# Transposed probabilities of the relation layers move into the attention's two PSUM banks

## The chip, the cores and the metric

One core of a Trainium2 chip runs the whole program. The metric is the device time of one execution in microseconds. The engines are TensorE (PE), VectorE (DVE), ScalarE (ACT), GpSimd (POOL) and SyncE (SP), which issues most transfers.

## What is computed

The input is 128 graphs of 128 nodes with 256 features and a 0/1 adjacency matrix each. They pass through one attention block and two relation layers:

```python
nx = ln(x); q, k, v = nx @ wq + bq, nx @ wk + bk, nx @ wv + bv      # 8 heads of 32
attn = softmax(q @ k.T / sqrt(32) + where(adj > 0, 0.1 * adj * adj, -inf))
x1 = x + (attn @ v) @ wo + bo
x = x1 + gelu(ln(x1) @ w1 + b1) @ w2 + b2                           # hidden width 1024
for l in range(2):                                                  # relation layers
    q, k = x @ Wq[l].T + bq[l], x @ Wk[l].T + bk[l]                 # width 128
    a = softmax(where(adj == 0, -1e10, q @ k.T / sqrt(128)))        # then 0 where adj == 0
    x = ln(x + (a @ x) @ Wc[l].T) * g[l] + b[l]
```

Most dense products are made as three matmuls of 16-bit halves (high by high, high by low, low by high), to come near fp32.

## The kernel before

Four graphs make a group, so there are NG = 32 groups. The work on a group is cut into steps named stage.step: N (first layer norm), Q (projections q0, q1, k0, k1, v0, v1), A (attention: S scores, max, exp, PT transposed probabilities, AV, each for graph 0 to 3, then oT, wo, and st, rs, xh of the second norm), M (MLP: mT, up0 to up7, lo, down0 to down7, x2), C0 and C1 (the two relation layers: xT, q, k, S, max, ex, xW, PT, PV, st, rs, xh, af).

It is a software pipeline. Every engine has a list of steps, each with an offset of groups ("C1.PT-4" is that step for the group four behind), and `run` goes through the list once for each group; after the last, a second list (`TENSOR_END` and so on) drains the pipeline. Each engine keeps strictly to its list, and waits on semaphores for what others make. The lists are all that sets the order of the work.

PSUM has eight banks. Banks 0 and 1 are the attention's (psA): A.S writes 8 heads of scores there, VectorE takes them away with the bias added (L872, d_S), A.PT transposes the exps into the same two banks (L1304), and ScalarE (L673) and VectorE (L880, d_PT) take those away as a high and a low half; A.wo writes them as well (taken away by L902, d_x1). Banks 2 and 3 serve Q, AV and up, 4 and 5 the MLP's output, and 6 and 7 the relation layers: q and S in bank 6, k in 7, xW and PV as rows in both.

In a relation layer, xW is x @ Wc and is copied to cW by ScalarE (L715). The exps (L709) are made in place in cs; PT transposes cs by TensorE (L1360) into bank 6 + l, ScalarE copies that back to cs (L719), and PV multiplies cs by cW (L1366). So either PT needs cW copied away first. VectorE scales and adds the residual in C0.PV and C1.PV (L955).

What each step of TensorE must wait for so that its banks are free stands in `freed` calls: freed(g, (signal, behind, per, k)) waits until `signal` has come k times for the group `behind` places before g. Other lines that the text names: L688 gelu (L691 its high half, L334 its low half, by VectorE for even and POOL for odd pieces), L667 exps of the attention, L681 high half of mT, L921 x2, L749 and L754 statistics, L762 normalised rows, L544 and L546 the reciprocal root on POOL, L551 row additions on POOL, L1297 A.S, L1348 C.S, and L327 to L329, the three matmuls of a product of any kind. rot is what A.wo and M.up read, cT what C.q, C.k and C.xW read; SyncE's transfers transpose into them.

## Time and profile before

| | us |
|---|---|
| median of 3 runs | 2076.52 |
| lowest, highest | 2076.26, 2077.35 |
| the profiled execution's own time | 2075.52 |
| its span | 2073.3 |
| mean granted TensorE clock | 0.976 |

The profile is one execution; times in its rows are from the span's start. TensorE is busy for 1868.7 of 2073.3 us, VectorE for 1701.3, ScalarE for 1563.1 and POOL for 925.4. A row of a timeline gives start, duration, engine, line, operation and tiles; in brackets is the engine's idle time before it and what ended it. Matmuls overlap by about 0.17 us, so a TensorE step makes room for the next one somewhat before its row ends.

### The profile page before, as it was taken

The numbers are of one execution on the slowest core, as the hardware profiler recorded it, in microseconds if no ns is written. First come the engines' busy times: TensorE is split into PE (matmuls) and PEld (weight loads), VectorE is DVE, ScalarE is ACT, GpSimd is POOL, SyncE is SP. The second block draws the span as 40 slices with busy tenths as digits, with TensorE's granted clock in tenths as the row PEclk, the third lists the DMA queues.
The fourth block names the chain that finished last, engine by engine and source line by source line (L and its number), as shares of the span: only waits on it lengthen the run. The fifth ranks groups of instructions, "written<-read, shape, count | busy, mean of one in ns | idle before, by whom it ended". The sixth has DMA issues, their size and how long they took to land.

```text
span 2073.3 us, 44187 instructions
## 1 busy us (share of the span) xinstructions
PE 1868.7 (90%) x15704; PEld 1347.0 (65%) x15704; DVE 1701.3 (82%) x3402; ACT 1563.1 (75%) x2996; POOL 925.4 (45%) x1168
## 2 busy tenths in 40 slices
...
PEclk8788899999999999999999999999999999999998
...
DMA packets 441657, 192.45 MB, mean 93 GB/s; under 512 B 347808, under 2 KB 416416, under 8 KB 441440
## 3 DMA queue, kind: packets, MB, share of 16 engines
...
q8 instruction: 128, 2.10, 0.4%
q0 software_dynamic: 544, 0.80, 0.2%
...
## 4 chain that ended last, share of the span: by engine, by line
PE 60%; ACT 18%; DVE 10%; POOL 5%; issue 4%; DMA 1%; SPq 1%; ACTq 0%; DVEq 0%; POOLq 0%
PE ps L327 16%; PE ps L329 16%; PE ps L328 16%; PE ps L1304 6%; ACT area L667 4%; PE ps L1366 3%; DVE st L749 2%; ACT L688 2%; DVE area L762 2%; ACT cs L709 2%; POOL hid_l L334 2%; DVE area L902 2%; ACT L709 2%; POOL rs L546 2%; POOL ve L544 2%
## 5 line engine op out<-in xcount | busy, mean ns | idle before, releaser
L544 POOL TENSOR_TENSOR ve<-mv,eps_cols 128x4 f32<-128x4 f32 x128 | 64.1, 500 | 738.5 <-DVE mv L754 738.5
L667 ACT ACTIVATE area<-area,nmax 128x128 f32<-128x128 f32 x1024 | 312.6, 390 | 17.0 <-DVE nmax L877 16.2
L327 PE MATMUL ps<-w_h,hid_h 128*128 128x256 f16 x1024 | 279.5, 273 | 12.1 <-POOL hid_l L334 12.1
L334 POOL TENSOR_TENSOR hid_l<-area,hid_h 128x512 f16<-128x512 f32 x128 | 156.4, 1222 | 279.1 <-ACT hid_h L691 279.1
L328 PE MATMUL ps<-w_l,hid_h 128*128 128x256 f16 x1024 | 279.3, 273 | 0.0
L329 PE MATMUL ps<-w_h,hid_l 128*128 128x256 f16 x1024 | 279.2, 273 | 0.0
L688 ACT ACTIVATE area<-ps,b_col 128x512 f32<-128x512 f32 x256 | 176.1, 688 | 41.0 <-PE ps L329 37.9
L327 PE MATMUL ps<-rot_h,w_h 128*128 128x512 f16 x512 | 198.5, 388 | 8.4 <-ACT area L688 5.3
L328 PE MATMUL ps<-rot_l,w_h 128*128 128x512 f16 x512 | 198.0, 387 | 0.0
L329 PE MATMUL ps<-rot_h,w_l 128*128 128x512 f16 x512 | 197.9, 387 | 0.0
L880 DVE SCALAR_TENSOR_TENSOR pT<-ps,pT 128x1024 f16<-128x1024 f32 x128 | 156.1, 1220 | 20.1 <-ACT pT L673 20.1
L551 POOL TENSOR_TENSOR x<-x,cb_row 128x256 f32<-128x256 f32 x240 | 167.3, 728 | 4.7
L858 DVE SCALAR_TENSOR_TENSOR qk<-ps,bqk_col,qk 128x512 f16<-128x512 f32 x128 | 95.6, 747 | 84.2 <-ACT qk L656 84.2
L691 ACT CAST hid_h<-area 128x512 f16<-128x512 f32 x256 | 158.2, 618 | 8.2
L872 DVE SCALAR_TENSOR_TENSOR area<-ps,biasA 128x1024 f32<-128x1024 f32 x128 | 154.9, 1211 | 5.3 <-PE ps L1297 5.3
L877 DVE TENSOR_REDUCE nmax<-area 128x8 f32<-128x1024 f32 x128 | 155.4, 1214 | 2.2
L673 ACT ACTIVATE pT<-ps 128x1024 f16<-128x1024 f32 x128 | 130.3, 1018 | 25.3 <-PE ps L1304 25.3
L1304 PE MATMUL ps<-ident,area 128*128 128x128 f32 x1024 | 138.3, 279 | 11.4 <-ACT area L667 6.7
L1366 PE MATMUL ps<-area,cs 128*128 128x256 f32 x512 | 125.2, 388 | 20.3 <-ACT cs L719 19.1
L1304 PEld LDWEIGHTS ps<-ident,area 128*128 128x128 f32 x1024 | 117.9, 144 | 33.6 <-issue 17.4
L697 ACT CAST sC_h<-area 128x1024 f16<-128x1024 f32 x32 | 33.4, 1045 | 137.8 <-DVE area L921 137.8
L546 POOL TENSOR_TENSOR rs<-ve,minus_half 128x4 f32<-128x4 f32 x128 | 132.7, 1036 | 10.0
...
## 6 DMA issues: line engine op xcount, KB each, us to landing
...
rot_h<-sA_h SPq DMA_TRANSPOSE x64, 2.8
rot_l<-sA_l SPq DMA_TRANSPOSE x64, 2.7
```

The lines of the kernel that those rows point to most:

```text
L327: pe.matmul(dst, lh, rh, start=start, stop=False, **kw)
L328: pe.matmul(dst, lh, rl, start=False, stop=False, **kw)
L329: return pe.matmul(dst, ll, rh, start=False, stop=stop, **kw)
L334: eng.tensor_tensor(hid_l[:, c % RING, :], hidden[:, c % 2, :], hid_h[:, c % RING, :], ALU.subtract).then_inc(done, 1)
L546: pool.tensor_tensor(rs[:, n], ve[:, n], minus_half[:, :], ALU.pow).then_inc(p_rs[n], 1)
L551: last = pool.tensor_tensor(dst[:, b], src[:, b], row, op)
L667: last = act.activation(sc[:, b % 2, h], sc[:, b % 2, h], ACT.Exp, bias=nmax[:, b, h:h + 1])
L688: act.activation(hidden[:, b % 2, :], psUp, ACT.Gelu, bias=b1_col[:, b:b + 1], scale=1.0 / W_SCALE).then_inc(a_gelu, 1)
L691: act.copy(hid_h[:, b % RING, :], hidden[:, b % 2, :]).then_inc(a_hi, 1)
L880: dve.scalar_tensor_tensor(pT16[:, b % 2, 1], psA_heads, P_SCALE, pT16[:, b % 2, 0], ALU.mult, ALU.subtract).then_inc(d_PT, 1)
L1304: last = pe.transpose(psA_heads[:, h], sc[:, b % 2, h], ident[:, :])
L1366: last = pe.matmul(rows_of(l, g)[:, b], cs[:, l, b], places(l, g)["cW"][:, b], start=True, stop=True)
```

## The change

The transposed probabilities of both relation layers go into bank l (0 or 1), the attention's, in place of bank 6 + l; a new helper `turned` gives the place to TensorE's transpose and ScalarE's copy. C0.PT and C1.PT then wait for the attention's last use of the bank, and no more for cW; A.wo and A.S1 wait for the copies out of it (a_cPT). For C1.PT in the steady lists that last use is A.S0 of the group four ahead of it (d_S), for C0.PT it is A.PT3 of the group two ahead (d_PT). All ten order lists are written anew, and the waits of TensorE with them. One piece of VectorE's preparation for the first group moves from Q.mA to A.S0.

```diff
--- before.py
+++ after.py
@@ -49,66 +49,67 @@
 
 
 
-TENSOR = ["M.down2-2", "M.up6-2", "Q.q0+0", "A.S3-1", "C0.S-3", "Q.q1+0", "A.AV0-1", "M.down3-2",
-          "A.PT2-1", "A.AV1-1", "M.down4-2", "Q.k1+0", "A.AV2-1", "A.PT3-1", "C0.xW-3", "A.AV3-1",
-          "M.up7-2", "C0.PT-3", "M.down5-2", "C0.PV-3", "M.down6-2", "M.down7-2", "A.wo-1",
-          "C1.q-4", "C1.k-4", "C1.S-4", "Q.v1+0", "Q.v0+0", "A.S0+0", "C1.xW-4", "C1.PT-4",
-          "A.S1+0", "M.up0-1", "C1.PV-4", "M.up1-1", "A.PT0+0", "M.up2-1", "M.down0-1", "M.up3-1",
-          "M.down1-1", "C0.q-2", "A.S2+0", "M.up4-1", "Q.k0+1", "C0.k-2", "A.PT1+0", "M.up5-1"]
-SCALAR = ["M.up2-2", "A.PT0-1", "M.up3-2", "A.exp1-1", "M.up4-2", "Q.k0+0", "A.PT1-1", "M.up5-2",
-          "C0.q-3", "C0.k-3", "M.up6-2", "Q.q0+0", "A.exp2-1", "Q.q1+0", "C1.xT-4", "A.PT2-1",
-          "A.exp3-1", "Q.k1+0", "A.PT3-1", "C0.ex-3", "C0.xW-3", "A.oT-1", "C0.PT-3", "M.up7-2",
-          "C0.xT-2", "C1.q-4", "C1.k-4", "Q.v1+0", "M.mT-1", "C1.ex-4", "C1.xW-4", "A.exp0+0",
-          "C1.PT-4", "M.up0-1", "Q.v0+0", "M.up1-1", "N.xT+1"]
-VECTOR = ["C1.max-5", "M.mT-2", "A.S0-1", "A.max0-1", "M.mC-3", "Q.v1-1", "N.st+0", "C0.st-4",
-          "A.S1-1", "N.xh+0", "M.lo0-2", "A.max1-1", "N.xT+0", "C1.PV-5", "A.PT0-1", "Q.v0-1",
-          "C1.st-5", "M.lo2-2", "A.S2-1", "A.max2-1", "C0.xh-4", "Q.k0+0", "C1.xh-5", "M.lo4-2",
-          "A.PT1-1", "Q.q0+0", "C0.S-3", "A.S3-1", "A.AV0-1", "A.max3-1", "C0.max-3", "Q.q1+0",
-          "A.AV1-1", "A.PT2-1", "C1.xT-4", "Q.k1+0", "A.AV2-1", "A.PT3-1", "A.AV3-1", "A.oT-1",
-          "M.lo6-2", "Q.mA+0", "C0.PV-3", "M.x2-2", "A.wo-1", "A.st-1", "C0.xT-2", "C1.S-4",
-          "A.xh-1"]
-GPSIMD = ["N.rs+1", "C0.rs-3", "M.lo1-1", "C1.rs-4", "M.lo3-1", "C1.af-4", "A.x1b-1", "M.lo5-1",
-          "C0.af-3", "M.lo7-1", "N.xb+0", "A.rs+0"]
-SYNC = ["C1.xT-4", "A.oT-1", "Q.stk+0", "M.ldC-2", "N.ld+1", "M.mT-1", "C0.xT-2", "Q.ldA+1",
-        "N.xT+1", "C1.sto-4"]
+TENSOR = ["M.up6-2", "M.down3-2", "A.S3-1", "A.AV0-1", "C0.S-3", "Q.q1+0", "A.AV1-1", "A.PT2-1",
+          "M.down4-2", "Q.k1+0", "A.AV2-1", "A.PT3-1", "C0.xW-3", "A.AV3-1", "C0.PT-3", "M.up7-2",
+          "M.down5-2", "C0.PV-3", "M.down6-2", "M.down7-2", "A.wo-1", "C1.k-4", "Q.v1+0", "C1.q-4",
+          "Q.v0+0", "C1.S-4", "A.S0+0", "C1.xW-4", "C1.PT-4", "A.S1+0", "M.up0-1", "C1.PV-4",
+          "A.PT0+0", "M.up1-1", "C0.k-2", "M.up2-1", "A.S2+0", "M.up3-1", "M.down0-1", "M.down1-1",
+          "M.up4-1", "M.down2-1", "Q.k0+1", "A.PT1+0", "M.up5-1", "C0.q-2", "Q.q0+1"]
+SCALAR = ["A.exp0-1", "M.up0-2", "A.PT0-1", "M.up1-2", "N.xT+0", "M.up2-2", "C1.xT-4", "M.up3-2",
+          "A.exp1-1", "M.up4-2", "Q.k0+0", "C0.k-3", "A.PT1-1", "M.up5-2", "Q.q0+0", "C0.q-3",
+          "M.up6-2", "A.exp2-1", "Q.q1+0", "A.PT2-1", "A.exp3-1", "Q.k1+0", "A.PT3-1", "C0.ex-3",
+          "C0.xW-3", "C0.PT-3", "A.oT-1", "M.up7-2", "C1.k-4", "C0.xT-2", "Q.v1+0", "C1.q-4",
+          "Q.v0+0", "M.mT-1", "C1.ex-4", "C1.xW-4", "C1.PT-4"]
+VECTOR = ["M.mT-2", "A.S0-1", "A.max0-1", "C0.xh-4", "N.st+0", "M.mC-3", "A.S1-1", "C1.PV-5",
+          "M.lo0-2", "N.xh+0", "A.PT0-1", "A.max1-1", "Q.v0-1", "N.xT+0", "C1.st-5", "M.lo2-2",
+          "A.S2-1", "Q.k0+0", "A.max2-1", "C1.xh-5", "M.lo4-2", "A.PT1-1", "Q.q0+0", "A.S3-1",
+          "A.AV0-1", "A.max3-1", "C0.S-3", "A.AV1-1", "Q.q1+0", "C0.max-3", "A.PT2-1", "C1.xT-4",
+          "A.AV2-1", "Q.k1+0", "A.PT3-1", "M.lo6-2", "A.AV3-1", "A.oT-1", "C0.PV-3", "Q.mA+0",
+          "M.x2-2", "C0.st-3", "A.wo-1", "A.st-1", "C0.xT-2", "Q.v1+0", "A.xh-1", "C1.S-4",
+          "C1.max-4"]
+GPSIMD = ["M.lo1-1", "C1.rs-4", "M.lo3-1", "N.xb+1", "C1.af-4", "A.x1b-1", "M.lo5-1", "C0.af-3",
+          "M.lo7-1", "C0.rs-2", "A.rs+0", "N.rs+2"]
+SYNC = ["N.ld+0", "M.ldC-3", "M.mT-2", "C0.xT-3", "N.xT+0", "Q.ldA+0", "C1.sto-5", "C1.xT-4",
+        "A.oT-1", "Q.stk+0"]
 
 QK = ("q0", "q1", "k0", "k1")
...
+TENSOR_END = ["A.AV0-1", "A.S3-1", "C0.S-3", "M.down3-2", "C0.xW-3", "A.PT2-1", "M.down4-2",
+              "A.AV1-1", "M.up6-2", "A.AV2-1", "A.PT3-1", "C1.k-4", "C1.q-4", "A.AV3-1", "M.up7-2",
+              "C0.PT-3", "M.down5-2", "C0.PV-3", "M.down6-2", "C1.S-4", "M.down7-2", "A.wo-1",
+              "C1.xW-4", "C1.PT-4", "C1.PV-4", "C0.k-2", "C0.q-2", "M.up0-1", "C1.k-3", "M.up1-1",
+              "C0.S-2", "M.up2-1", "M.down0-1", "M.up3-1", "C0.xW-2", "M.up4-1", "M.down1-1",
+              "C0.PT-2", "M.down2-1", "M.up5-1", "C1.q-3", "M.up6-1", "M.down3-1", "M.up7-1",
...
@@ -281,6 +282,9 @@
 
         def keys_of(l, g, n):
             return bank_of(l, g, n).rearrange("p (b k) -> p b k", b=B)
+
+        def turned(l):
+            return ps[:, l, :].rearrange("p (b k) -> p b k", b=B)
 
         def rows_of(l, g):
             first = ROWS_LAST[l] if number(g) == NG - 1 else places(l, g)["bank"]
@@ -716,7 +720,7 @@
                         elif what == "PT":
 
                             need(act, t_cPT[l], g, 1, 1)
-                            act.copy(cs[:, l], keys_of(l, g, l)).then_inc(a_cPT[l], 1)
+                            act.copy(cs[:, l], turned(l)).then_inc(a_cPT[l], 1)
 
             run(SCALAR, SCALAR_END, iteration)
 
@@ -777,7 +781,7 @@
                     assert made[0] == BQK_MADE, made[0]
                     prep(dve.tensor_copy(bv_rep, bv_col[:, :].unsqueeze(2).broadcast_to([P, KC, P])))
                     prepped()
-                elif step == "Q.mA":
+                elif step == "A.S0":
                     lows(HALVES_QKV, HALVES_QKVO)
                     dve.wait_ge(ld_vec, 16 * NVEC)
                     prep(dve.tensor_copy(cb_rep, cln_col[:, 1, :].unsqueeze(2).broadcast_to([P, KC, P])))
...
+                    elif step == "C0.PT":
+                        freed(g, (d_PT, -2, 4, 4), (d_x1, -1, 1, 1), (a_cPT[0], 1,
+                              1, 1))
...
                     elif step == "A.wo":
+                        freed(g, (a_cPT[0], 2, 1, 1), (d_PT, 0, 4, 4))
                         freed(g, (d_PT, 0, 4, 4))
...
                     elif step == "C1.PT":
-                        freed(g, (a_cW[1], 0, 1, 1))
+                        freed(g, (d_S, -4, 4, 1), (d_x1, -3, 1, 1), (a_cPT[1], 1, 1,
+                              1))
                     elif step == "A.S1":
                         freed(g, (d_S, 0, 4, 1))
+                        freed(g, (a_cPT[1], 4, 1, 1), (d_S, 0, 4, 1))
...
                     elif step == "C1.PV":
                         freed(g, (a_cW[1], 0, 1, 1))
-                        freed(g, (a_cPT[1], 0, 1, 1))
+                    elif step == "A.PT0":
+                        freed(g, (d_S, 0, 4, 2))
...
+                    elif step == "A.S2":
+                        freed(g, (d_PT, 0, 4, 1))
...
@@ -1357,7 +1363,7 @@
                         elif what == "PT":
                             for b in range(B):
                                 need(pe, a_cexp[l], g, B, b + 1)
-                                last = pe.transpose(keys_of(l, g, l)[:, b], cs[:, l, b], ident[:, :])
+                                last = pe.transpose(turned(l)[:, b], cs[:, l, b], ident[:, :])
                             last.then_inc(t_cPT[l], 1)
                         elif what == "PV":
                             need(pe, a_cPT[l], g, 1, 1)
```

In the end lists (the rest is left out above) C1.k, C1.q and C1.S of the fourth last group stand before A.wo of the last, and C1.PV of it and C0.k and C0.q of the second last group before M.up0 of the last; before, they all stood behind.

## Rows read from the trace of the kernel before

**Rows 1.** The page: busy us and shares; clock granted, in tenths
```profile
PE 1868.7 (90%) x15704; PEld 1347.0 (65%) x15704; DVE 1701.3 (82%) x3402; ACT 1563.1 (75%) x2996; POOL 925.4 (45%) x1168
...
PEclk8788899999999999999999999999999999999998
```

**Rows 2.** Chain of work in order of time: start, us, what
```profile
1063.39 1.24 DVE area L902
...
1123.83 1.24 DVE area L902
```

**Rows 3.** TensorE's waits, 400 to 1800: us in total, times, longest
```profile
PE ps L1360 <- ACT area L715: 40.0, 23, 2.0
PE ps L1348 <- ACT ck L702: 20.9, 24, 0.9
PE ps L1366 <- ACT cs L719: 13.9, 23, 0.7
PE ps L327 <- POOL hid_l L334: 9.4, 23, 0.4
```

**Rows 4.** Timeline of TensorE: start, us, line, operation, idle before
```profile
1075.36 0.66 PE L1360 MATMUL ps<-ident,cs 128*128 128x128 f32 x4 [1.73 <-ACT area L715]
...
1076.30 0.38 PE L327 MATMUL ps<-rot_h,w_h 128*128 128x512 f16 x1
...
1078.37 0.89 PE L1366 MATMUL ps<-area,cs 128*128 128x256 f32 x3 [0.61 <-ACT cs L719]
...
1088.94 0.61 PE L1297 MATMUL ps<-qkS 96*128 96x128 f16 x8
...
1121.01 0.27 PE L327 MATMUL ps<-wo_h,rot_h 128*128 128x256 f16 x1
```

**Rows 5.** Timeline of ScalarE, same group
```profile
1070.39 1.05 ACT L681 CAST sA_h<-area 128x1024 f16<-128x1024 f32 x1 [0.52 <-DVE area L762]
...
1071.46 1.28 ACT L709 ACT_TABLE_LOAD   x1
...
1077.55 0.57 ACT L719 COPY cs<-ps 128x512 f32<-128x512 f32 x1
...
1080.15 0.62 ACT L691 CAST hid_h<-area 128x512 f16<-128x512 f32 x1
...
1101.54 2.45 ACT L667 ACTIVATE area<-area,nmax 128x128 f32<-128x128 f32 x8
```

**Rows 6.** Timeline of VectorE, same group
```profile
1061.05 1.23 DVE L921 SCALAR_TENSOR_TENSOR area<-ps,area 128x1024 f32<-128x1024 f32 x1
...
1063.39 1.23 DVE L902 SCALAR_TENSOR_TENSOR area<-ps,xin 128x1024 f32<-128x1024 f32 x1 [1.12 <-PE ps L329]
...
1068.98 1.38 DVE L762 TENSOR_SCALAR area<-area,mv,rs 128x256 f32<-128x256 f32 x4 [0.31 <-POOL rs L546]
...
1072.62 1.22 DVE L872 SCALAR_TENSOR_TENSOR area<-ps,biasA 128x1024 f32<-128x1024 f32 x1
...
1081.98 0.68 DVE L334 TENSOR_TENSOR hid_l<-area,hid_h 128x512 f16<-128x512 f32 x1
...
1087.23 1.21 DVE L880 SCALAR_TENSOR_TENSOR pT<-ps,pT 128x1024 f16<-128x1024 f32 x1
```

**Rows 7.** Timeline of POOL, same group
```profile
1066.66 1.09 POOL L544 TENSOR_TENSOR ve<-mv,eps_cols 128x4 f32<-128x4 f32 x1 [4.72 <-DVE mv L754]
...
1077.93 0.20 POOL L544 TENSOR_TENSOR ve<-mv,eps_cols 128x4 f32<-128x4 f32 x1 [9.09 <-DVE mv L754]
...
1097.16 3.16 POOL L551 TENSOR_TENSOR x<-x,cg_row 128x256 f32<-128x256 f32 x4 [3.43 <-DVE x L762]
...
1118.28 1.35 POOL L334 TENSOR_TENSOR hid_l<-area,hid_h 128x512 f16<-128x512 f32 x1 [4.63 <-ACT hid_h L691]
```

**Rows 8.** The page: transfer issues, with us from issue to landing
```profile
rot_l<-sA_l SPq DMA_TRANSPOSE x64, 2.7
```

**Rows 9.** Timeline of TensorE in the last groups
```profile
1979.91 1.54 PE L1360 MATMUL ps<-ident,cs 128*128 128x128 f32 x4 [3.01 <-ACT cs L709]
```

174 lines of the change are left out of this document (76 added, 98 removed), and 26 rows, old and new, of tables (SCALAR_END, VECTOR_END).

## The prediction

> **What bounds the kernel now.** I read the page first: TensorE is busy 90% of the span and its granted clock is at 90% or more of full speed (the 2.4 GHz level) from the sixth of 40 slices to the last but one, so TensorE sets the pace [rows 1]. Then the chain of work: the residual after the output projection (L902, step A.wo of VectorE) comes once per group of four graphs, 60.44 us apart [rows 2]. There are 32 groups, so 31 such distances, of which I count 30 as steady. Then TensorE's waits over 1400 us, 23 groups: 84.2 us in four kinds, 3.66 us a group [rows 3]. Each ends a pipeline that has to fill again (about 0.16 us, the overlap of two neighbours), so 4.3 of 60.44 us are lost and 56.1 us are TensorE's own work. The largest wait, 1.73 us, is the one this change attacks: the transposes of the second relation layer (C1.PT, L1360) stand behind ScalarE's copy of cW (L715), because they share its bank [rows 3, 4].
>
> In what follows T is the time from the start of A.wo on TensorE, 1060.57 in the trace; the next one starts at 1121.01, T 60.44 [rows 4]. TensorE's own pace: the six 512-column matmuls of M.up0 start at 1076.30 and end 0.61 before 1078.37, the last of them lasting 0.38, so 0.216 us from start to start; the 24 of 256 columns of A.wo are done 2.8 us after 1121.01, when L902 starts, 0.109 each [rows 2, 4]. So q, k, up, Q.* take 1.30, a down or half of Q.v 1.31, A.wo and xW 2.62; from start differences, A.S 0.45, C.S 0.95, C.PT 0.50, A.PT 0.9, AV 0.60, PV 1.80.
>
> **The change, part by part.** No instruction is added or removed; all go by other lists, and two orderings change their banks.
>
> 1. *C1.PT into bank 1.* It no longer waits for cW, but for the evacuation of A.S0 (L872). And A.S1, which writes bank 1, now waits for ScalarE's copy of cs (L719). Queued behind A.S1 on TensorE is all the rest, M.up0 first. So the old wait (1.73) and the PV wait (0.61) are exchanged for a wait at A.S1, whose release is: transpose copy of A.xh 1.05, table load 1.28, four exps 1.56, cW 0.9, cs copy 0.57 [rows 5]. (The four exps and cW: from the table load's end, 1072.74, to the cs copy at 1077.55 are 4.81, less 2.35 for the eight exps of A.exp0 in between: 2.46.) Today M.up0 starts at T 15.73 (1076.30), after 12.8 of own work [rows 4].
>
> 2. *C0.st put between M.x2 and A.wo on VectorE.* Today VectorE idles 1.12 there [rows 6]. x2 can start at T 0.20 (last down ends, plus 0.04) instead of 0.48, since C0.PV is now ahead of Q.mA; x2 takes 1.14 to the next start, the statistics 1.41+0.14+0.30. A.wo goes to T 3.19 instead of 2.82: +0.37. From A.wo to A.xh are 5.59 us (1063.39 to 1068.98), statistics and the two POOL steps, 1.09 and the rsqrt behind it [rows 6, 7]; same neighbours, so A.xh at 8.78. C1.S and C1.max now follow it (0.69+0.03+0.61 before M.mT, which needs ScalarE's copy at 11.23 anyway): M.mT 11.40, A.S0 12.55. On ScalarE: copy 10.19 to 11.23, exps from 12.54, cW 14.1, cs copy 15.0 to 15.56, A.S1 15.62, M.up0 **16.07**, against 15.73. PV then goes at 17.37 without waiting (today 17.80), so 0.4 is gained here.
>
> 3. *A.S2 earlier.* It waits for VectorE's share of A.PT0 (L880), in a list that now reads A.S0, max0, C0.xh, N.st, mC, A.S1, C1.PV, lo0, N.xh, A.PT0. Today the stretch from A.S0 (1072.62) to the end of N.xh (1081.98) takes 9.36 [rows 6]; out of it go Q.v1 (0.60) and C0.st (1.81), into it come C0.xh (1.29, as N.xh), C1.PV (1.97), lo0 (0.60) and A.PT0 itself (1.21): 12.02. So 12.55 + 12.02 = 24.57, and with 0.05 to 0.14 of signal A.S2 starts at 24.62 to 24.71. TensorE would be there at 16.07 + 8.0 = 24.07 (up0, PV, PT0, up1, C0.k, up2). That is a new wait of 0.6, where today A.S2 comes four steps later (T 28.37) and finds its banks free.
>
> 4. *From A.S2 to exp2.* TensorE's own work to M.up6 is 13.1: up6 at 37.8. ScalarE: up6 ends 39.25, gelu 0.69 and cast 0.62 (with the gap 1.35: from the table load after the cs copy, over at 1079.42, to 1080.77), table load 1.28, exp2 2.45 with small gaps [rows 5]: exp2 done at 44.4, today 43.4 (1103.99). Then PT2 waits 0.15 (exp to TensorE takes 0.14), PT2's copy 45.5, exp3 to 48.95 and **A.PT3 at 49.1**, today 48.35. TensorE alone would be there at 48.65: a wait of 0.45.
>
> 5. *The end of the group.* From PT3 TensorE has xW, AV3, C0.PT, up7, down5, PV, down6, down7: 11.5 us, so A.wo at 60.65 if nothing waits. C0.PT moved ahead of up7 and its copy ahead of A.oT: the copy ends at 54.5, A.oT 55.45, table load 56.75, gelu and cast 58.1, lo7 on POOL (1.16 to 1.35, rows 7) 59.3 to 59.5. Today's wait before down7 (0.41) shrinks to 0 to 0.2. A.wo at **60.8**. So 60.44 becomes 60.8: +0.35 a group, ends +0.0 (if every hand-off falls at its short end and lo7 is hidden, with the PT0 step short) and +0.6.
>
> 6. *Moves that cost nothing.* N.xb goes to POOL's idle 3.4 us before C1.af [rows 7]; should that cover go, lo5 would come 2.78 late and down5 still has 6 us. ldC behind N.ld on SyncE, and N.xT later on VectorE: its transpose lands near 30.5, read at 31.7. The transpose that M.up0 reads takes 2.7 to land [rows 8]: issued near 12.85, it is there at 15.6, before 16.07; this is the nearest cover of all, and if it went, up0 would come later by what it overshoots. Six table loads a group, as before. DVE's preparation moves from Q.mA to A.S0, once.
>
> 7. *The last groups.* The end lists put C1.k, C1.q, C1.S(-4) ahead of A.wo(-1), and PV(-4), C0.k, C0.q(-2) ahead of M.up0(-1), a place where TensorE waits 3.01 for exps [rows 9]. From up0 to the last down the own work falls from 35.1 to 30.2 us; up0 starts some 2 us later, since C0.k needs C1.PV evacuated. I take −3, ends −6 and +2. The start: 0, ends ±2.
>
> Sum against the profiled execution, span 2073.3 and time 2075.52: 30 groups x 0.35 = +10.5, −3: +7.5, so 2083.0. The median shown, 2076.52, lies 1.0 above that execution; for it I say **2084**.
>
> **A rule weighed.** The row first: the same POOL addition on 128x4 took 1.09 us beside VectorE's C0.xT and 0.20 elsewhere [rows 7]; it ended when C0.xT did. The Trainium skill, page "SBUF — State Buffer", section "Who interferes with whom", says that whichever of the two engines issues first holds the shared ports for the whole instruction and the other blocks, here for a VectorE operation with two SBUF inputs; the trace agrees with 1.09 against 0.20. What that gives where POOL is first is the fourth rival.
>
> **The rivals.**
> *Faster.* The freed bank pays: VectorE's list is not late at A.S2, because x2 and the statistics hide in the 1.12 of idle time and the PT0 step is reached by T 24.0. The place is A.wo of VectorE, the price 0.37 plus the wait of 0.6; it decides if A.S2 starts under 24.1. Then 60.0 a group: 30 x −0.44 − 3 = −16: 2060.5. For it: waits of 1.73 and 0.61 do vanish. Against it: the chain x1 to A.xh has no slack.
> *Even.* The waits only trade places, 60.44 stays, and the end gives −3: 2073.5. For it: 4.3 lost today, 4.4 to 4.8 by my sum, less than my hand-offs can tell apart.
> *It doesn't do what it says:* C1.PT still stands behind cW's time, since A.S1 waits for the copy that ScalarE makes after cW. That is in the forecast.
> *Much slower.* lo1 on POOL is issued ahead of N.xh on VectorE (T 22.95 against 22.07 by my sum; it decides 0.9 earlier) and holds it for 1.16: A.S2 at 25.8, 30 x 1.45 − 3 = +40: 2117.
>
> **How the numbers follow.** Forecast 0.50, faster 0.20, even 0.24, much slower 0.06. The forecast's own range is 2077 to 2092; with even and half of faster I give 2062 to 2092, which leaves 0.10 below and 0.08 above. Within 0.2% (4 us, about what can be told from no change) lies 0.14 of the forecast's 0.50 and 0.15 of even's 0.24, the other 0.09 being faster: faster 0.29, same 0.29, slower 0.42.
>
> **What would show it.** Right: L902 60.7 to 60.9 apart; C1.PT's wait on L715 gone; waits of L1297 on L719 (A.S1) of about 2 and on L880 (A.S2) of 0.4 to 0.7; L1304 on L667 0.3 to 0.5; L902 on VectorE with hardly any idle time before it. Wrong: A.S2 without a wait (step 3), a distance under 60.4, or a last stretch that is not shorter (step 7).

## The result and the profile after

The changed kernel takes 2094.27 us (median of 3 runs, 2094.0 to 2098.02) against 2076.52: a ratio of 1.0091, 95% interval 1.0075 to 1.0107. It is slower by 17.75 us, where +7.5 was forecast and 2092 was the top of the range. Its profiled execution took 2094.0 us, span 2091.1, at nearly the same mean granted clock (0.974 against 0.976). That mean hides two places where TensorE's clock stands at half (0.50 of full, the 1.2 GHz level): once for 3.4 us among the middle groups, where the kernel before has none, and for 10.2 us instead of 3.4 in the last groups. Both come up below. The page, with the clock in tenths as in [rows 1]:

```profile
PE 1892.6 (91%) x15704; PEld 1354.8 (65%) x15704; DVE 1671.9 (80%) x3402; ACT 1566.5 (75%) x2996; POOL 928.6 (44%) x1168
...
PEclk8699899999999999999999999999999999999998
```

The code has moved by 4 to 6 lines: L902 is now L906, L1360 is L1366 (C.PT), L1297 is L1303 (A.S), L1304 is L1310 (A.PT), L1366 is L1372 (C.PV), L872 is L876, L880 is L884, L719 is L723 and L327 to L329 are L331 to L333. The chain of work (start, us, what) answers [rows 2]:

```profile
641.84 1.12 DVE area L906
702.76 1.12 DVE area L906
...
1191.42 1.19 DVE area L906
1246.89 2.73 DMA rot_l<-sA_l
1252.57 1.24 DVE area L906
```

The first pair is 60.92 us apart. The second is 61.15 apart, and here a transfer has come into the chain: the low half of the transpose that A.wo reads. In the chain of the kernel before it does not occur between 500 and 1700 us. TensorE's waits from 400 to 1800 us answer [rows 3]:

```profile
PE ps L1303 <- issue: 25.1, 23, 1.1
PE ps L331 <- DVE cs L940: 23.4, 23, 1.5
PE ps L1310 <- DVE area L876: 7.4, 22, 0.7
PE ps L1310 <- ACT area L671: 7.3, 23, 0.3
PE ps L1303 <- DMA qkS<-qk: 5.5, 9, 0.9
PE ps L1366 <- DVE area L876: 4.4, 23, 0.2
PE ps L331 <- DMA rot_l<-sA_l: 4.4, 9, 0.9
```

C1.PT's wait for the copy of cW (40.0 us) is gone, as intended. In its place A.S1 waits 1.09 us in each group; the profile names no releaser ("issue"), but in the group of A.wo at 699.43, whose other rows stand further below, ScalarE's cs copy ends at 715.01 and A.S1 starts at 715.11:

```profile
714.45 0.56 ACT L723 COPY cs<-ps 128x512 f32<-128x512 f32 x1
```

C1.xW waits for VectorE's evacuation of C1.S (L940), A.PT0 for that of A.S1, and in 9 of 23 groups A.wo waits for its transpose. All in all TensorE waits for fewer microseconds, but more often: 77.7 us in 133 waits, against 84.2 us in 93 [rows 3]. Its busy time is 23.9 us longer with the same instructions, so part of what is lost stands inside its busy rows: A.wo at 1127.45, for instance, starts 0.38 us behind the matmul before it, where neighbours in that row are 0.11 apart, and no wait is listed.

I took the starts of A.wo from the traces (31 distances). By them the 17.5 us between the two last A.wo starts (1966.0 and 1983.5) are: 1.1 before the first A.wo, 186.6 to 183.2 = −3.4 over the first three distances, +19.1 over the next 27, +0.7 in the last. So the middle groups are 0.71 longer each (mean 60.47 to 61.18). The commonest distance goes from 60.44 to 60.91, so 0.47 or 0.48 of this is the base, and 0.23 come from groups above it. (In the changed kernel only 7 of 27 groups stand at 60.91 to 60.93; four are shorter.) From the last A.wo to the end it is 107.3 and 107.7: the last groups gave nothing.

### The profile page after: what moved, and what is told of

The parts are those of the page before. It is cut to its first block, busy times and chain, and to the rows that moved or that the text cites. A ratio compares the mean times of both kernels' runs of the same rounds, so it can differ in the third digit from the quotient of the medians.

```text
span 2091.1 us, 44128 instructions
## 1 busy us (share of the span) xinstructions
PE 1892.6 (91%) x15704; PEld 1354.8 (65%) x15704; DVE 1671.9 (80%) x3402; ACT 1566.5 (75%) x2996; POOL 928.6 (44%) x1168
## 4 chain that ended last, share of the span: by engine, by line
PE 53%; DVE 25%; issue 7%; ACT 6%; POOL 3%; DMA 3%; SPq 2%; DVEq 0%; ACTq 0%; POOLq 0%
PE ps L331 14%; PE ps L333 14%; PE ps L332 14%; PE ps L1310 6%; DVE st L753 5%; ACT area L671 4%; DVE area L876 3%; DVE area L766 2%; DVE area L906 2%; PE ps L1372 2%; DVE xh L959 2%; DMA rot_l<-sA_l 2%; DVE xh L766 2%; POOL rs L550 2%; POOL ve L548 2%
## 5 line engine op out<-in xcount | busy, mean ns | idle before, releaser
L338 POOL TENSOR_TENSOR hid_l<-area,hid_h 128x512 f16<-128x512 f32 x128 | 149.3, 1166 | 302.3 <-ACT hid_h L695 302.3
L331 PE MATMUL ps<-w_h,hid_h 128*128 128x256 f16 x1024 | 279.4, 273 | 1.0 <-POOL hid_l L338 1.0
L333 PE MATMUL ps<-w_h,hid_l 128*128 128x256 f16 x1024 | 279.1, 273 | 0.0
L331 PE MATMUL ps<-rot_h,w_h 128*128 128x512 f16 x512 | 197.0, 385 | 10.4 <-ACT area L692 3.4
L333 PE MATMUL ps<-rot_h,w_l 128*128 128x512 f16 x512 | 196.8, 384 | 0.0
L706 ACT ACTIVATE ck<-ps,cb_col 128x512 f32<-128x512 f32 x61 | 41.6, 682 | 206.3 <-PE ps L333 206.3
L884 DVE SCALAR_TENSOR_TENSOR pT<-ps,pT 128x1024 f16<-128x1024 f32 x128 | 156.3, 1221 | 40.5 <-ACT pT L677 40.5
L555 POOL TENSOR_TENSOR x<-x,cb_row 128x256 f32<-128x256 f32 x240 | 179.8, 780 | 4.7
L876 DVE SCALAR_TENSOR_TENSOR area<-ps,biasA 128x1024 f32<-128x1024 f32 x128 | 156.0, 1219 | 20.6 <-PE ps L1303 17.2
L1310 PE MATMUL ps<-ident,area 128*128 128x128 f32 x1024 | 141.7, 283 | 25.1 <-DVE area L876 13.1
L331 PE MATMUL ps<-cw_h,cT_h 128*128 128x256 f16 x488 | 133.3, 273 | 29.4 <-DVE cs L940 29.4
L1310 PEld LDWEIGHTS ps<-ident,area 128*128 128x128 f32 x1024 | 116.9, 145 | 49.5 <-DVE area L876 26.9
L1303 PE MATMUL ps<-qkS 96*128 96x128 f16 x1024 | 81.1, 224 | 67.3 <-issue 30.6
```

What stands on the lines that cost most here:

```text
L331: pe.matmul(dst, lh, rh, start=start, stop=False, **kw)
L333: return pe.matmul(dst, ll, rh, start=False, stop=stop, **kw)
L338: eng.tensor_tensor(hid_l[:, c % RING, :], hidden[:, c % 2, :], hid_h[:, c % RING, :], ALU.subtract).then_inc(done, 1)
L555: last = pool.tensor_tensor(dst[:, b], src[:, b], row, op)
L876: dve.scalar_tensor_tensor(sc[:, b % 2], psA_heads, 1.0 / QK_SCALE, biasA[:, b].unsqueeze(1).broadcast_to([P, H, P]), ALU.mult, ALU.add).t ...
L884: dve.scalar_tensor_tensor(pT16[:, b % 2, 1], psA_heads, P_SCALE, pT16[:, b % 2, 0], ALU.mult, ALU.subtract).then_inc(d_PT, 1)
```

## The experiments

T is again the time from A.wo's start. In the texts put down ahead of each run, T1 is the theory under test, R1 and R2 its rivals. Line numbers of the experiments are off by up to 6 from those above. The table holds all kernels; the distance is that of A.wo's starts over the 27 middle groups, commonest and mean.

| kernel | us | ratio to before, 95% | distance |
|---|---|---|---|
| before | 2076.52 | 1 | 60.44; 60.47 |
| changed | 2094.27 | 1.0091 (1.0075 to 1.0107) | 60.91; 61.18 |
| e1_oT_first | 2110.55 | 1.0178 (1.0155 to 1.0201) | none; 61.88 |
| e2_st_late | 2159.75 | 1.0405 (1.0391 to 1.0419) | 62.79; 63.32 |
| e3_both | 2190.92 | 1.0556 (1.0534 to 1.0579) | none; 64.95 |
| e4_end_swap | 2093.38 | 1.0081 (1.0065 to 1.0097) | 60.91; 61.21 |
| e5_lists_old_banks | 2118.79 | 1.0204 (1.0191 to 1.0218) | 61.90; 61.98 |
| e6_banks_only | 2195.93 | 1.0578 (1.0563 to 1.0592) | 64.84; 64.84 |
| e7_banks_act | 2075.59 | 0.9999 (0.9990 to 1.0008) | 60.44; 60.51 |
| e8_own_turned_rows | 2093.05 | 1.0083 (1.0066 to 1.0100) | 60.92; 61.06 |
| e9_short_st | 2092.86 | 1.0088 (1.0074 to 1.0101) | 60.91; 61.29 |
| e11_both | 2090.84 | 1.0077 (1.0064 to 1.0090) | 60.92; 60.98 |
| e12_less_st | 2088.9 | 1.0060 (1.0047 to 1.0073) | none; 60.90 |
| e13_own_less_st | 2080.71 | 1.0023 (1.0014 to 1.0032) | 60.51; 60.69 |
| e14_before_table | 2072.39 | 0.9985 (0.9976 to 0.9994) | 60.35; 60.38 |
| e15_banks_act_table | 2062.04 | 0.9931 (0.9917 to 0.9944) | 59.88; 59.99 |
| e16_after_table | 2093.89 | 1.0088 (1.0074 to 1.0101) | 60.92; 61.17 |

**The transposes, by reordering.** My theory was that two things lengthen the group: C0.st ahead of A.wo's evacuation on VectorE, and transposes that come too late. SyncE's queue just ahead of A.wo (start, us to issue), first of before, A.wo at 1121.01:

```profile
1112.77 1.25 SPq L429 DMA_TRANSPOSE cT_h<-sC_h  x1
...
1116.88 1.25 SPq L432 DMA_TRANSPOSE rot_l<-sA_l  x1
```

then of the changed kernel, A.wo at 1127.45 (the one before at 1066.48):

```profile
1119.44 1.25 SPq L433 DMA_TRANSPOSE cT_h<-sC_h  x1
1120.79 2.11 SPq L436 DMA_TRANSPOSE cT_l<-sC_l  x1
1123.09 1.30 SPq L433 DMA_TRANSPOSE rot_h<-sA_h  x1
1124.50 1.25 SPq L436 DMA_TRANSPOSE rot_l<-sA_l  x1
```

Four transposes are issued one after the other. The first must wait until C0.xW has read the shared cT tiles (T 52.2 before, 53.0 now); the last needs 2.7 us to land [rows 8]. Before, rot_l was issued 4.13 us ahead of A.wo, 1.4 to spare. Now the row starts 0.8 later, and one of the issues took 2.11 instead of 1.24, so that A.wo waited. By the landings in the trace, A.wo starts 1.36 us behind that of rot_l in most of the first groups of the kernel before, and 0.87 in the changed one. Where the transfer decides, it starts 0.14 behind it: so it is at 5 of the 27 middle distances before, and at the last 16 of the 27 in the changed kernel.

```diff
-SYNC = [..., "C1.sto-5", "C1.xT-4", "A.oT-1", "Q.stk+0"]
+SYNC = [..., "C1.sto-5", "A.oT-1", "C1.xT-4", "Q.stk+0"]
```

> One edit to the changed kernel: in SyncE's list of the steady groups the two transposes of the attention's output (A.oT) are issued before the two of C1's rows (C1.xT), not behind them. T1, transposes come too late: in the second half of the changed kernel's groups A.wo waits up to 0.9 us for rot_l, and those groups take 61.1 to 61.5 us against 60.91 in the groups where it doesn't wait. With the edit that wait is gone, every group takes 60.9, some 27 x 0.23 = 6 us less: about 2088 us, ratio to the kernel before 1.005 to 1.006. R1, the wait for the transposes only stands where another chain would have made TensorE wait anyway (VectorE's late bias addition C0.st, which is absorbed in those groups): groups stay at 61.1, and the time at 2094 (ratio 1.009). R2, C1's transposes, now later, feed C1.xW and C1.q: if they bind, TensorE waits for xT_l at the head of C1 and the time goes above 2094.

A miss: slower than the changed kernel. A.oT's source is ready only near T 56, so that C1.xT, which had used the time ahead of it, now stands behind it, and with it the twelve loads of the staged Q and K (qkS), 7.7 to 9.3 us of issue. A.S0 waits for them. SyncE's queue in one group of e1:

```profile
1077.04 1.46 SPq L433 DMA_TRANSPOSE cT_h<-sC_h  x1
...
1080.51 9.16 SPq L482 DMA_DIRECT2D qkS<-qk  x12
```

and TensorE's largest wait there:

```profile
PE ps L1303 <- DMA qkS<-qk: 54.5, 23, 3.8
```

These are 54.5 us of waits, where the changed kernel has 5.5. Part of the loss is TensorE's clock: in 7 of the 27 groups it stands at half for 3.4 or 6.8 us, in five of them inside or just behind this wait of A.S0 (up to 3.8 us). These groups take 63.5 on the average, the other 20 take 61.3. None of the theories had named that neighbour: R2 looked at C1's own readers. SyncE's queue is tight on both sides of A.oT.

**C0.st, by reordering.**

```diff
-VECTOR = ["M.mT-2", "A.S0-1", "A.max0-1", "C0.xh-4", "N.st+0", "M.mC-3", "A.S1-1", "C1.PV-5", ...,
-          "M.x2-2", "C0.st-3", "A.wo-1", ...
+VECTOR = ["M.mT-2", "A.S0-1", "A.max0-1", "C0.st-4", "A.S1-1", "N.st+0", "M.mC-3", "C0.xh-4",
+          "C1.PV-5", ..., "M.x2-2", "A.wo-1", ...
```

The edit also moves C0.xh behind M.mC, GpSimd's C0.rs behind A.rs, and C0.st in the last groups (not shown).

> Edit to the changed kernel: on VectorE C0.st goes out of the place between M.x2 and A.wo to behind A.max0, A.S1 follows it at once, C0.xh goes behind M.mC, GpSimd makes C0.rs after A.rs; in the last groups the same step moves. SyncE's order stays that of the change. T1: A.wo's evacuation comes 0.4 us earlier and A.PT0 no longer waits for A.S1's (7.4 us in 23 groups), but the wait for the transposes in front of A.wo is the next one to bind in every group, so the gain is small: groups of 60.8 to 61.1, 2088 to 2092 us (ratio 1.006 to 1.0075). R1, the transposes bind nothing: every group loses the 0.37 us that step 2 of the prediction put on it, groups of 60.5, about 2081 (ratio 1.002).

> Both edits together: the attention's transposes first on SyncE, and C0.st later on VectorE. T1, the longer group is the sum of those two: groups of 60.5 us, 30 x 0.45 = 13 us less than the changed kernel: about 2079 to 2081, ratio 1.0015. R1, a third term keeps it up (the wait of A.S1 for ScalarE's copy of the transposed probabilities, 25.1 us of TensorE's waits in 23 groups, 1.09 each): groups stay at 60.8 to 60.9 and the time at 2087 or above (ratio 1.005).

Both missed by far. The waits of e2:

```profile
PE ps L331 <- DVE x L959: 42.3, 22, 2.3
...
PE ps L1303 <- DVE pT L884: 15.9, 17, 1.1
```

C0.st came before C1.PV's evacuation (L959), which C0.k waits for, in a stretch where VectorE has no idle time; 1.9 us of it appear at once as C0.k's wait, and the rest at A.S2. In e3 the two damages more than add up (64.95, where the sum would be 64.02): in 20 of its 27 groups, and in 6 of e2's, the granted clock stands at half for 3.4 or 6.8 us. In the groups without that, e3 has 63.46, e2 63.12 and e1 61.31, and there they do add up. The new order of e2 costs 1.9 in its commonest group (62.79 less 60.91), although the 0.4 in front of A.wo is saved. These three runs refute nothing about the two causes: they replaced them by larger ones.

**The two causes, taken away rather than moved.** For the transposes C1 gets cT tiles of its own, so that SyncE need not wait for C0.xW:

```diff
+        c1_h, c1_l = sb("c1_h", [P, KC, R], F16), sb("c1_l", [P, KC, R], F16)
...
+        second = dict(shared, cT_h=c1_h, cT_l=c1_l)
...
-            return own if late(l, g) else shared
+            return own if late(l, g) else second if l == 1 else shared
...
+                        if l == 1 and number(g) < LATE:
+                            need(sp, t_cW[1], g, 1, 0)
...
```

> Edit to the changed kernel: C1's transposed rows get tiles of their own (4 KB a partition more) in the steady groups, so that C1.xT's two transposes no longer wait until C0.xW has read the shared tiles (53 us after A.wo's start) and go out before the attention's. SyncE's order is kept. T1 (transposes too late): rot_l lands over a microsecond before A.wo wants it in every group, the 4.4 us of waits in 9 groups go, groups of 60.9 throughout, about 2088 us (ratio 1.0055 to 1.0065). R1, the waits for rot_l only take the place of waits on other engines: groups stay at 61.1 and the time at 2094 (ratio 1.009). R2, SyncE's later queue (qkS, the staged Q and K) sets A.S0 even so: its wait stays in 9 groups, and about half of the 6 us is gained.

For C0.st three quarters of its work are left out (its time goes, its place stays):

```diff
+                batches = 1 if n == 2 and 4 <= number(g) < NG - 4 else B
-                for b in range(B):
+                for b in range(batches):
...
```

> Edit to the changed kernel: in groups 4 to 27 C0's statistics (C0.st) are made of one of the four batches only, so 3 BATCH_NORM_STATS2 and 3 aggregates of each are left out (about 1.3 us of VectorE between M.x2 and A.wo's evacuation); the other three batches keep older statistics. T1 (C0.st ahead of A.wo's evacuation costs 0.37 us where rot_l doesn't bind): A.wo's evacuation starts at 2.8 instead of 3.2 us, C1.xW at 10.4 instead of 10.8; groups without a wait for rot_l fall to 60.5, but the transposes then bind in nearly all of them, since they have no more room, and the groups settle near 60.8 to 61.1: 2088 to 2092 us (ratio 1.006 to 1.008). R1, nothing changes (A.S1's wait for the cs copy sets the group): 2094, groups of 60.9. R2, all 1.3 us come back: groups below 60.0 and about 2066.

> Edit to the changed kernel: C1's turned rows in tiles of their own (in the steady groups) together with C0.st on one batch of four in groups 4 to 27 (3 statistics and 3 aggregates of each left out). T1, the changed group is longer by the late C0.st and by the late transposes: with both gone C1.xW is at 10.4, A.wo waits for nothing, groups of 60.5 us, as the kernel before: 24 x 0.37 = 9 us less than with the tiles alone, about 2083 us (ratio 1.003 to 1.004). R1, one of A.S1's wait for the cs copy (1.09 us), A.PT0's or A.PT3's sets it: groups of 60.9 and 2091 (ratio 1.007). R2, the wait for qkS takes the place: A.S0 later and C1.xW still at 10.8.

Two earlier runs were to do the same, with a condition on the group that matched none; nothing was left out, and their instructions are those of the changed kernel and of e8. They stand as repeats (1.0088 and 1.0077), and what they expected was not tried by them:

> Edit to the changed kernel: in the steady groups C0's statistics (C0.st) are made of one of the four batches only, 3 BATCH_NORM_STATS2 and 3 aggregates left out, about 1.3 us of VectorE between M.x2 and A.wo's evacuation; the statistics of the other three batches are left as they were. T1 (step 2 of the prediction, C0.st ahead of A.wo costs 0.37 us a group): A.wo's evacuation starts 2.8 us after A.wo instead of 3.2, C1.S and C1.xW come 0.37 earlier, and in the groups that don't wait for rot_l the period falls to about 60.55; in the others the transposes bind already and nothing is gained. About 2086 to 2090 us (ratio 1.0045 to 1.0065). R1, C0.st costs nothing there (A.S1's wait for the cs copy or the transposes set the group): 2094, ratio 1.009. R2, VectorE is short of time all through the group, and all 1.3 us come back: groups below 60.0 and about 2070.

> Both edits together to the changed kernel: C1's transposed rows in tiles of their own, and C0.st on one batch of four. T1, late transposes and the late C0.st together make nearly all of the difference to the kernel before: groups of 60.5 us, about 2080 to 2082 (ratio 1.002 to 1.003). R1, a third term of the same size (A.S1's wait for ScalarE's copy of the transposed probabilities): groups at 60.9 and 2088 or more (ratio 1.006).

Measured, the waits for SyncE's transfers, 400 to 1800 us (L333 and L331 are the matmuls, L1308 is A.S). In e8:

```profile
PE ps L1308 <- DMA qkS<-qk: 5.0, 9, 0.9
...
PE ps L333 <- DMA rot_l<-sA_l: 0.3, 1, 0.3
```

In e12:

```profile
PE ps L331 <- DMA rot_l<-sA_l: 3.0, 9, 0.6
```

And in e13:

```profile
PE ps L333 <- DMA rot_l<-sA_l: 1.3, 3, 0.9
```

With tiles of their own the wait for rot_l all but goes (4.4 to 0.3), and 21 of 27 distances are 60.91 or 60.92; but the mean falls by 0.11 only, and the time by less than the interval can tell (T1's 2088 is missed). Its two longest groups (61.96 and 61.93) are the two with 3.4 us at half clock. With C0.st shortened the commonest 60.91 is gone, and waits for rot_l stay, as T1 of e12 had it (2088.9). With both the distance is 60.51, 0.07 from before, and the time 2080.7 (T1 had 2083): 1.2 and 5.4 us apart from the changed kernel one by one, 13.6 together. That is what two limits side by side look like: where the transposes are late, C0.st is hidden, and the other way round. The changed kernel's own trace has both in turn. Through its first twelve middle groups A.S1 starts at T 15.7 (16.0 twice), as with C0.st ahead of A.wo's evacuation. The other fifteen begin with an A.wo that came 0.14 us behind its transpose, and in them A.S1 starts at T 15.3 to 15.5, as in e12 and e13: VectorE had made up the 0.4 while TensorE waited.

**The banks and the lists apart.** e5 is the changed kernel with the old banks in the steady groups; e6 is the kernel before with the new banks and the waits for them; e7 is e6 with one swap on ScalarE:

```diff
-          "C0.xT-2", "C1.q-4", "C1.k-4", "Q.v1+0", "M.mT-1", "C1.ex-4", "C1.xW-4", "A.exp0+0",
-          "C1.PT-4", "M.up0-1", "Q.v0+0", "M.up1-1", "N.xT+1"]
+          "C0.xT-2", "C1.q-4", "C1.k-4", "Q.v1+0", "M.mT-1", "C1.ex-4", "C1.xW-4", "C1.PT-4",
+          "A.exp0+0", "M.up0-1", "Q.v0+0", "M.up1-1", "N.xT+1"]
```

> The changed kernel's order lists with the steady groups' transposed probabilities in the old banks (C0.PT in bank 6, C1.PT in bank 7, waits for them as in the kernel before); the last groups keep the new banks. T1, the longer group comes from the lists (C0.st between M.x2 and A.wo, C1.PT and A.S1 close together, transposes): the time is that of the changed kernel within 4 us (2090 to 2098, ratio 1.007 to 1.0105), with A.S1's 1.09 us wait moved to C1.PT, C1.PV or M.up0. R1, the banks themselves cost (A.S1 waiting for the cs copy, A.S2 for PT0): without them the groups fall to 60.5 and the time to about 2081 (ratio 1.002). R2, the lists need the new banks: C1.PT, now waiting for ScalarE's copy of cW, comes over a microsecond later and the time goes above 2110.

> The kernel before with the banks of the change alone: in the steady groups the transposed probabilities go into banks 0 and 1, with waits for them, in the old order lists. T1, the banks need the lists: A.S1 follows C1.PT in bank 1 and now waits for ScalarE's cs copy, which the old list has behind A.exp0 (5 us), so M.up0 starts near 18 instead of 15.7 us after A.wo; some of it is caught up, groups of 62.2 to 62.8, 2125 to 2145 us (ratio 1.024 to 1.033). R1, C1.PT no longer waits for ScalarE's cW copy (40.0 us of waits in the middle of the kernel before) and this pays for it: 2070 to 2080. R2, A.S1's wait is absorbed by up1, which waits for its GELU anyway: groups of 60.5 to 61.

> As the run before, and one more edit: ScalarE makes the cs copy (C1.PT) ahead of A.exp0. T1, A.S1 waits about 1 us for the copy, in place of C1.PT's old wait of 1.7 us for the cW copy: M.up0 at 15.7 as in the kernel before, while A.exp0, 0.57 us later, makes A.PT0 or M.up1 later by up to 0.2: groups of 60.4 to 60.7, 2076 to 2084 us (ratio 1.000 to 1.004). R1, the wait that is gone is a gain: groups under 60.3, below 2072 (ratio under 0.998). R2, the copy ahead of A.exp0 holds the chain of exponentials and GELUs up by its whole 0.57 us: groups of 61.0, 2093.

TensorE's largest waits in e5 (L1364 is C.PT, of both layers):

```profile
PE ps L1364 <- ACT area L719: 46.6, 45, 1.6
```

In e6 (L1302 is A.S):

```profile
PE ps L1302 <- ACT cs L722: 74.5, 22, 3.4
```

In e7, the second row being M.up1's wait for its gelu:

```profile
PE ps L1302 <- ACT cs L722: 24.2, 23, 1.1
...
PE ps L330 <- ACT area L691: 16.1, 23, 0.7
```

Neither half of the change stands without the other: the lists with old banks are 24.5 us slower than with new ones (R2 of e5), and the banks with old lists cost 4.4 us a group. A.S1 waits 3.4 there for a cs copy that stands behind A.exp0, which is T1's mechanism, but the price is nearly twice T1's (2196 against at most 2145). The rest of it is TensorE's clock. In each of e6's 27 middle groups the granted clock stands at half for 6.8 us, from T 16.8 in most, inside A.S1's wait; its mean over the run is 0.934. One such group of e6, first a row of `--windows` for that stretch (the third figure from the end, 0.50, is the clock), then TensorE's timeline:

```profile
1133.20:1140.00 6.80, 6.04 (x21) 4.04 (x22) 5.48 (x19) 3.78 (x6) 2.52 (x4) 0.50 0.22 58
```

```profile
1133.96 1.04 PE L1302 MATMUL ps<-qkS 96*128 96x128 f16 x8 [3.38 <-ACT cs L722]
...
1137.35 3.20 PE L1371 MATMUL ps<-area,cs 128*128 128x256 f32 x8
```

A.S1 takes 1.04 us there instead of 0.61, C1.PV 3.20 instead of 1.89, and the matmuls of M.up0 are 0.43 apart instead of 0.22. Counted from start to start over all 27 groups, these three steps take 2.7 us a group longer than in the kernel before, listed waits left aside. That leaves 1.7 for the waits, about what T1 had put on them (62.2 to 62.8).

One swap on ScalarE removes all of it, and e7 is the kernel before to 0.1%, with no stretch at half clock in its middle groups. There C1.PT's 1.73 has shrunk to 0.26 (A.S0's evacuation) and PV's 0.61 is gone, and A.S1 waits 1.05 and M.up1 0.70 for its gelu: the waits trade places, as the rival "even" had it. So the banks cost nothing, and the 18 us are the new lists'.

**Why a removed wait brings nothing.** In e7, as in the kernel before, ScalarE works from C1.ex to beyond exp2 with idle moments of 0.4 us at most, and C1.ex starts only when its table load is over [rows 5]. If ScalarE sets the pace, moving that load into idle time must show. One instruction does it:

```diff
+                    if stage + "." + what == "Q.v1" and order is SCALAR:
+                        act.activation(warm[:, :], minus_half[:, :], ACT.Exp)
```

> The kernel before with one instruction more a group: a tiny exponential of a constant (128x4, into a tile of its own) on ScalarE before its evacuation of Q.v1, where ScalarE stands idle for 2.6 us. The table load for exponentials (1.28 us), which now stands in front of C1.ex from 10.9 to 12.2 us after A.wo's start, would then fall into that idle time. T1 (what holds both banks' versions at 60.44 is ScalarE, busy without a break from C1.ex to the last GELU): C1.ex starts 0.6 to 1.3 us earlier, cW's copy is then bound by C1.xW's end (13.1), C1.PT waits 0.6 us less, and the groups fall by 0.3 to 0.7 us to 59.8 to 60.1: 2055 to 2067 us (ratio 0.990 to 0.996). R1, M.up0's transposes (landed at 15.6) or the work behind 20 us hold the group: 60.4, same time. R2, the chip loads a table again at C1.ex, so that the added one only costs: same time or up to 2 us more.

> The version with the new banks in the old order, the cs copy ahead of A.exp0, and the early table load. T1: the cW copy and then the cs copy come 0.6 us earlier, A.S1's wait for the copy falls from 1.05 to about 0.5 us, M.up1's wait for the GELU from 0.7 to 0.1; groups of 59.8 to 60.0, 2055 to 2062 us (ratio 0.990 to 0.993), 0 to 5 us below the kernel before with the same early load, since here nothing waits for cW's copy any more. R1, the transposes of A.mT (landed at 15.6) hold M.up0, so that only the second wait shrinks: the same as the other, within 2 us.

> The changed kernel with the early table load (the tiny exponential before ScalarE's evacuation of Q.v0). T1: C1.ex ends earlier, but A.S1 still waits for cW's copy and then the cs copy, which start when C1.xW and C1.PT end on TensorE (13.4 and 14.2 us after A.wo): A.S1's wait falls by 0.3 to 0.7 us, and the rest of the group gains that where rot_l doesn't bind: 2080 to 2092 us (ratio 1.002 to 1.0075). R1, the rest of the group is set by SyncE's transposes and staged loads: no change, 2093. R2, ScalarE's idle time before A.mT is 1.2 us there, too short for the load: A.mT's copy is late and its transposes too: 2095 to 2105.

ScalarE in e15, A.wo at 995.50:

```profile
1001.61 1.28 ACT L653 ACT_TABLE_LOAD   x1
1002.91 0.20 ACT L653 ACTIVATE warm<-minus_half 128x4 f32<-128x4 f32 x1
...
1005.32 1.04 ACT L687 CAST sA_h<-area 128x1024 f16<-128x1024 f32 x1 [0.52 <-DVE area L768]
1006.27 0.40 ACT L715 ACTIVATE cs<-cs,cmax 128x128 f32<-128x128 f32 x1
...
1008.60 1.02 ACT L721 ACTIVATE area<-ps 128x1024 f32<-128x1024 f32 x1 [0.68 <-PE ps L333]
1009.52 0.58 ACT L725 COPY cs<-ps 128x512 f32<-128x512 f32 x1
```

C1.ex follows M.mT's copy at once, 1.4 us earlier than in e7 (T 10.77 against 12.18), and ScalarE now waits for C1.xW (0.68). With the new banks the group is 59.88 and the time 2062.0, 0.7% under the kernel before: the fastest of all, with the whole computation in it. With the old banks and the old order the same load brings only 0.09 a group (2072.4). R1 names this result, but the rows give another reason: A.exp0 then waits for its maximum (0.43 us) and the cs copy, behind A.exp0, starts at T 16.9 as before. e15 differs from e14 in two things, the banks and the cs copy's place ahead of A.exp0, where it fills that wait. The place alone, with the old banks, was not run. By e14's rows C1.PT starts at T 14.18 there, behind the copy of cW, so that a cs copy in front of A.exp0 would hold it up beyond its present 14.55, and I would expect no gain; this is argued, not shown. TensorE's waits in e14, C1.PT and PV:

```profile
PE ps L1363 <- ACT area L718: 26.7, 24, 1.1
...
PE ps L1369 <- ACT cs L722: 17.2, 23, 0.8
```

and in e15, A.S1 and M.up1:

```profile
PE ps L1305 <- ACT cs L725: 16.3, 24, 0.7
...
PE ps L331 <- ACT area L694: 8.1, 23, 0.4
```

In the changed kernel it brings nothing (R1 again, 2093.9). There A.S1 starts 0.43 earlier (T 14.87 against 15.30 in groups of the same start), and A.PT0 waits 0.43 longer for VectorE (0.75 against 0.32): in this stretch it is VectorE that holds the group, not ScalarE. And at the last 16 of its 27 middle distances A.wo again starts 0.14 us behind its transpose, as R1 had it. One group of the changed kernel, A.wo at 699.43; the timeline of TensorE:

```profile
713.24 0.79 PE L1366 MATMUL ps<-ident,cs 128*128 128x128 f32 x4 [0.19 <-DVE area L876]
715.11 0.61 PE L1303 MATMUL ps<-qkS 96*128 96x128 f16 x8 [1.09 <-issue]
...
719.06 1.09 PE L1310 MATMUL ps<-ident,area 128*128 128x128 f32 x8 [0.32 <-DVE area L876]
724.07 0.62 PE L1303 MATMUL ps<-qkS 96*128 96x128 f16 x8
```

and of VectorE:

```profile
702.68 1.19 DVE L906 SCALAR_TENSOR_TENSOR area<-ps,xin 128x1024 f32<-128x1024 f32 x1
...
708.22 1.38 DVE L766 TENSOR_SCALAR area<-area,mv,rs 128x256 f32<-128x256 f32 x4 [0.40 <-POOL rs L550]
...
717.79 1.22 DVE L876 SCALAR_TENSOR_TENSOR area<-ps,biasA 128x1024 f32<-128x1024 f32 x1
...
722.79 1.22 DVE L884 SCALAR_TENSOR_TENSOR pT<-ps,pT 128x1024 f16<-128x1024 f32 x1
```

From A.xh (708.22) to A.PT0's share (722.79) and beyond VectorE has no idle time, and A.wo's evacuation has none before it. Whatever makes that one later (C0.st by 0.4) comes out at A.S1's evacuation and the end of the group.

**The last groups.** In the new end list VectorE does C1.xh-3, which waits for GpSimd, before C0.S-1 and C0.max-1:

```diff
-              "C1.st-3", "C1.xT-2", "C1.xh-3", "C0.S-1", "C0.max-1", "C0.PV-1", ...
+              "C1.st-3", "C1.xT-2", "C0.S-1", "C0.max-1", "C1.xh-3", "C0.PV-1", ...
```

> One edit to the changed kernel, in the last groups alone: VectorE does C0's evacuation of scores and its maximum of the last group (C0.S-1, C0.max-1) before C1.xh-3, which waits for GpSimd, as the kernel before did. T1, the 3 us that the new last groups save are given back there (C0.PV of the last group starts 11.34 us after C0.k, before 9.40): 1.9 us less, about 2092.3, ratio 1.0082 against 1.0091, and in the trace those 11.34 us go to about 9.4. R1, the last 20 us are set by C1's chain (C1.xh-3, then C1 of the two last groups), which is later then: the interval shrinks and the end doesn't move (2094, or up to 1 us more).

The last C0.PT in the changed kernel's timeline:

```profile
2048.53 1.39 PE L1366 MATMUL ps<-ident,cs 128*128 128x128 f32 x4 [1.49 <-ACT cs L713]
```

and in e4's:

```profile
2048.38 1.06 PE L1366 MATMUL ps<-ident,cs 128*128 128x128 f32 x4
```

The wait is gone, and from the last A.wo to the end it is 105.2 instead of 107.7 us. (Some of these 2.5 us may be the clock: near the end it stands at half for 6.8 us in e4 and for 10.2 in the changed kernel.) The medians (2093.38 against 2094.27) lie 0.9 apart, and an interval of 3 us to either side can't tell T1's 1.9 from nothing: the trace shows the mechanism, the times don't confirm its size.

## Why the prediction missed

The direction and the mechanism of the base were right, the size was not, and step 6 put at nothing a term that was not nothing.

Steps 1 and 2 came out within 0.06 us. Group of A.wo at 699.43: A.wo's evacuation at T 3.25 (3.19 in the sum), A.xh 8.79 (8.78), A.S1 15.68 (15.62). The wait in front of A.S1 is 1.09 and not about 2, since C1.xW, which comes before it, has already waited about 1.0 for the evacuation of C1.S, which the sum didn't list as a wait. The even rival's reading of the banks alone is what e7 shows.

Step 3: A.S2 starts at T 24.64, inside 24.62 to 24.71, yet without the wait named there. TensorE had lost its time earlier, 0.32 us at A.PT0, waiting for A.S1's evacuation, which my list of VectorE contained and whose consumer I had not checked. e12 and e13 show that this stretch is carried by VectorE. The wait of A.S2 on L880, one of the prediction's own signs, isn't there.

Steps 4 and 5: A.PT3 at 49.31 (49.1, wait 0.32 for 0.45), A.wo at 60.91 (60.8). The base is +0.47 or 0.48 a group for +0.35, inside its ends: 27 x 0.125 = 3.4 us of the miss.

Step 6 is where it failed. It lists SyncE's moves as free and names the cover of the transpose for M.up0, but not that of A.wo's: 1.4 us before, and used up by 0.8 of later start (C0.xW ends later) and now and then a slow issue. The mean over the middle groups is 0.23 above the base: 27 x 0.23 = 6.2 us. Group by group, the excess over 60.91 is 3.7 us in fifteen of the sixteen groups that end with an A.wo bound by its transpose, 2.1 us in the sixteenth, and 1.4 us in the first eleven, where rot_l binds nothing (7.2 in all; the kernel before has 0.8 over its 60.44, which leaves about the 6.2). The sixteenth (from 1800.03, 63.02 us) is the cover that step 6 did name, giving out once: rot_l took 4.2 us to land instead of 2.7, M.up0 waited 0.78 for it, and TensorE's clock then fell to half for 3.4 us, with C1.PV at 2.70 us where it takes 1.89:

```profile
1818.90 2.70 PE L1372 MATMUL ps<-area,cs 128*128 128x256 f32 x8
```

e8 shows the wait to be removable, and e12 and e13 show that it and C0.st stand side by side, so that only both together bring the time back.

Step 7: 30.2 us were forecast from M.up0 to the last down, and it took 30.2 (2002.32 to 2032.55). But M.up0 came 18.9 us after the last A.wo (15.2 before), 3.6 later where some 2 was forecast, and C0.S behind C1.xh-3 gave 1.5 back at C0.PT: of −3 nothing was left, the end is 0.4 longer. The sum took TensorE's work at full clock, and much of what the new list puts ahead of M.up0 ran at half: 10.2 us there, for 3.4 before. C1.PV, before and after the change:

```profile
1983.75 1.89 PE L1366 MATMUL ps<-area,cs 128*128 128x256 f32 x8
```

```profile
1992.63 3.75 PE L1372 MATMUL ps<-area,cs 128*128 128x256 f32 x8 [0.95 <-ACT cs L723]
```

With the last distance (+0.7) that is 4.1 us. The start went the other way: 30 x 0.35 had put +1.05 on the first three distances, and up to there the changed kernel is 2.3 ahead (−3.4 and +1.1), which is 3.4 less. So 3.4 + 6.2 + 4.1 − 3.4 = 10.3, the 10.25 us between 7.5 and 17.75.

Of the rivals, "even" is true of the banks (e7), not of the lists. "Faster" fell with the point it named: A.S2 starts at 24.6, not under 24.1. POOL's lo1 did not hold up N.xh: in the group above VectorE goes from lo0 to N.xh without a gap.

What stays open: e13 is still 0.23% above the kernel before. Its commonest distance is 0.07 longer, but 11 of its distances lie above 60.6: the first eight, where A.PT0 waits 0.6 to 0.7 for A.S1's evacuation in all but one, and three with waits for rot_l or for xT_l. Why the early groups wait longer at A.PT0, and why the slow issues come mostly late in the run, no row says. Which part of e13's rest is due to the list, and which to the 1.3 us of VectorE that e13 leaves out, wasn't tried apart.
